# Splitting the partial sums of layer 0 between TensorE and VectorE 8 : 8, and moving the harmonics into a PSUM bank

## The reference

```python
# layer 0
h = relu(edge_feat @ W1 + b1)
w = (h @ W2 + b2).reshape(e, 4, 8, 8)          # four 8x8 matrices per edge
s_e, v_e = s[src], v[src]                      # 8 scalars and 8x3 vectors
m0 = ALPHA * (einsum('ei,eio->eo', s_e * sh0, w_000)
              + C110 * einsum('eim,em,eio->eo', v_e, sh1, w_110))
m1 = ALPHA * (einsum('ei,em,eio->eom', s_e, sh1, w_011)
              + einsum('eim,eio->eom', v_e * sh0, w_101))
out = segment_sum(m, dst) + self interaction
x = layernorm(x + out)
```

## Time and profile before

| | |
|---|---|
| median of 3 runs | 4191.23 us (4188.38 to 4191.39) |
| profiled execution | 4180.82 us |
| its span | 4179.0 us |
| mean granted TensorE clock | 0.938 |
| busy: PE, DVE, POOL, ACT | 86%, 79%, 72%, 53% |

### The profile page before, as it was taken

The page is one execution under the profiler, slowest core; times in us unless marked ns, Lnnn a source line. Parts: engine busy times, 40 slices in busy tenths (PEclk is TensorE's granted clock), DMA queues, the critical chain, the costliest instruction groups (busy, mean ns, idle before and its releaser), DMA issues.

```text
span 4179.0 us, 79599 instructions
## 1 busy us (share of the span) xinstructions
PE 3584.4 (86%) x24746; PEld 2173.1 (52%) x24746; DVE 3311.0 (79%) x5246; ACT 2201.5 (53%) x6573; POOL 3017.6 (72%) x3143
## 2 busy tenths in 40 slices
PE   5888888888888888888649999999999999999995
PEld 3555555555555555555425555555555555555553
DVE  7777777777777777777749988888888889888887
ACT  3555555555555555555325555555555556555553
POOL 5777777777777777777367777777777777777772
PEclk8999999999999999999879999999999999999998
DMA  3111111111111111111132212121212212121212
GB/s 103 33 29 33 29 33 29 34 33 29 33 29 33 29 33 29 33 31 31 18 48 47 46 39 47 37 47 37 47 37 47 47 37 48 37 47 37 47 37 32
DMA packets 220966, 159.83 MB, mean 38 GB/s; under 512 B 125489, under 2 KB 194994, under 8 KB 220466
## 3 DMA queue, kind: packets, MB, share of 16 engines
q0 software_dynamic: 100352, 51.58, 8.8%
q1 hardware_dynamic: 84946, 90.16, 8.2%
q10 hardware_dynamic: 35650, 17.88, 1.6%
HBM read 148.94 MB, written 10.43 MB: 38 GB/s over the span
## 4 chain that ended last, share of the span: by engine, by line
POOL 58%; issue 25%; PE 7%; DVE 6%; DMA 3%; DVEq 1%; POOLq 0%; ACT 0%; SPq 0%; ACTq 0%
POOL rows L364 58%; PE red L687 4%; PE wps L674 2%; DMA rows<-x_rows,src 2%; DVE prod L984 1%; DVE q L1036 1%; DMA src<-in_src 1%; PE wps L667 1%; DVE t_a L1022 0%; DVEq L1064 0%; DVE table L1060 0%; POOLq L381 0%; DMA x_rows<-table 0%; PE acc L701 0%; DMA rows<-in_x,src 0%
## 5 line engine op out<-in xcount | busy, mean ns | idle before, releaser
L364 POOL DMA_INDIRECT rows<-x_rows,src x1568 | 1504.6, 960 | 567.2 <-issue 562.7
L364 POOL DMA_INDIRECT rows<-in_x,src x1568 | 1512.1, 964 | 507.9 <-issue 498.5
L687 PE MATMUL red<-prod,ident 128*128 128x336 f32 (+2 forms) x6272 | 1753.6, 436 | 0.0
L687 PEld LDWEIGHTS red<-prod,ident 128*128 128x128 f32 x6272 | 1145.9, 193 | 651.1 <-issue 189.5
L493 ACT ACTIVATE gap<-iota,slot_plan 128x128 bf16<-128x128 f32 x3136 | 943.7, 387 | 85.3 <-DVE t_b L1087 76.0
L984 DVE TENSOR_TENSOR prod<-wps,q 128x896 f32<-128x896 f32 x784 | 836.3, 1084 | 191.2 <-PE wps L674 175.9
L667 PE MATMUL wps<-bias_parts,ones 64*128 64x448 bf16 (+1 forms) x2352 | 463.6, 391 | 517.4 <-DVE prod L978 324.4
L674 PE MATMUL wps<-w_sb,hidden 64*128 64x256 f32 (+1 forms) x4704 | 903.8, 487 | 0.0
L511 ACT ACTIVATE sums<-red 128x336 f32<-128x336 f32 (+2 forms) x392 | 168.6, 430 | 1084.1 <-PE red L687 1083.1
L667 PEld LDWEIGHTS wps<-bias_parts,ones 64*128 64x128 bf16 x2352 | 114.5, 94 | 1039.6 <-DVE prod L978 422.1
L674 PEld LDWEIGHTS wps<-w_sb,hidden 64*128 64x128 f32 x4704 | 487.5, 204 | 70.4 <-issue 25.6
(11 more groups left out here) (125 smaller groups left out, 3117.4 us busy)
## 6 DMA issues: line engine op xcount, KB each, us to landing
mlp<-in_dist SPq DMA_DIRECT2D x196, 256.0 KB
mlp<-in_feat SPq DMA_DIRECT2D x98, 256.0 KB
rows<-in_x,src POOLq DMA_INDIRECT x1568
rows<-x_rows,src POOLq DMA_INDIRECT x1568
frames<-frame ACTq DMA_DIRECT2D x49, 144.0 KB
geo<-frames ACTq DMA_DIRECT2D x98, 72.0 KB
src<-in_src SPq DMA_DIRECT2D x196, 8.0 KB, 1.6
geo<-in_sh ACTq DMA_DIRECT2D x98, 32.0 KB, 1.7
```

The source lines that it names most:

```text
L364: nc.gpsimd.indirect_dma_start(out=rows[z][:, t, :], out_offset=None, in_=table_rows, in_offset=bass.IndirectOffsetOnAxis(ap=src_sb[z][:, ...
L687: ins = nc.tensor.matmul(red[:, bank * 512:bank * 512 + cols], ident[:], pr[:, i, :, a:b, :], start=(i == 0), stop=(i == MUL - 1))
```

## The change

In layer 0 PE now sums tiles 0 to 7 only, in one bank, and DVE sums tiles 8 to 15. The second bank of `red`, which layer 0 no longer uses for sums, holds the harmonics: ACT copies each slot's 64 columns there with `copy_geo`, as it did for layer 1's frames, and DVE reads them from there. `load_geo` waits for that copy in place of DVE's last use; the copy waits for the load and for DVE's last use, and stands between the second half of the distances and the one-hots. DVE's first body waits until both slots are copied. Layer 1 keeps its split (12 : 4), its two banks and its place for the frames. `make_frames` stays where it is.

```diff
-PE_SUMS = (((0, 8), (8, 12)), ((0, 6), (6, 12)))
-PE_TILES = 12
-DVE_TILES = TILES - PE_TILES
-BANKS = 2
+PE_SUMS = (((0, 8),), ((0, 6), (6, 12)))
+PE_TILES = (8, 12)
+BANKS = (1, 2)
...
-        geo_ps = [hps[:, z * TILES * GEO[1]:(z + 1) * TILES * GEO[1]] for z in range(RING)]
-        red = psum("red", [P, BANKS * 512])
+        red = psum("red", [P, 2 * 512])
+        geo_ps = [[bank[:, z * TILES * GEO[n]:(z + 1) * TILES * GEO[n]] for z in range(RING)]
+                  for n, bank in enumerate((red[:, 512:1024], hps))]
...
-                act.wait_ge(s.geo_used[z] if n == 0 else s.geo_copied[z], r)
+                act.wait_ge(s.geo_copied[z], r)
...
-            def copy_geo(z, r):
+            def copy_geo(n, z, r):
-                s = layers[1]
+                s = layers[n]
                 act.wait_ge(s.geo_loaded[z], r * 16 + 16)
                 act.wait_ge(s.geo_used[z], r)
-                nc.scalar.activation(geo_ps[z], geo_sb[z][:], ACT.Copy).then_inc(s.geo_copied[z], 1)
+                nc.scalar.activation(geo_ps[n][z], geo_sb[z][:, 0:TILES * GEO[n]], ACT.Copy).then_inc(s.geo_copied[z], 1)
...
                     if n == 0:
+                        if not last:
+                            copy_geo(n, z, r + 1)
                         if not tail:
                             one_hots(n, z1, steps)
                             copy_sums(n, z1, r1, 0)
-                            copy_sums(n, z1, r1, 1)
...
                         weigh(n, z1, r1, range(2, H))
                         sum_products(n, z1, r1, 0)
-                        sum_products(n, z1, r1, 1)
...
             def harmonics(z):
-                return geo_sb[z][:, 0:TILES * GEO[0]].rearrange("p (t c) -> p t c", c=GEO[0])
+                return geo_ps[0][z].rearrange("p (t c) -> p t c", c=GEO[0])
...
-                if n == 0:
-                    dve.wait_ge(s.geo_loaded[z], r * 16 + 16)
-                else:
-                    dve.wait_ge(s.geo_copied[z], r + 1)
+                dve.wait_ge(s.geo_copied[z], r + 1)
...
             def prologue0(r, st):
+                dve.wait_ge(layers[0].geo_copied[1], r + 1)
```

More of the change, by code:

```diff
@@ L228, in __init__ @@
                 self.weights_used = ring("weights_used", HALVES[n])
-                self.products_summed = ring("products_summed", BANKS)
-                self.sums_copied = ring("sums_copied", BANKS)
+                self.products_summed = ring("products_summed", BANKS[n])
+                self.sums_copied = ring("sums_copied", BANKS[n])
                 self.messages_ready = ring("messages_ready")
@@ L252, in products @@
         def products(n):
-            return prod[:, 0:PE_TILES * PATHS[n] * MM].rearrange("p (i h t c) -> p i h t c", i=MUL, h=2 - n, t=PE_TILES)
+            return prod[:, 0:PE_TILES[n] * PATHS[n] * MM].rearrange("p (i h t c) -> p i h t c", i=MUL, h=2 - n, t=PE_TILES[n])
         def products_oi(n):
-            return prod[:, PE_TILES * PATHS[n] * MM:TILES * PATHS[n] * MM].rearrange(
-                "p (h t c i) -> p h t c i", i=MUL, h=2 - n, t=DVE_TILES)
+            return prod[:, PE_TILES[n] * PATHS[n] * MM:TILES * PATHS[n] * MM].rearrange(
+                "p (h t c i) -> p h t c i", i=MUL, h=2 - n, t=TILES - PE_TILES[n])
         def summed_by_dve(n, q):
-            return q * HALF_TILES[n] >= PE_TILES
+            return q * HALF_TILES[n] >= PE_TILES[n]
         def sums_by_half(n, z):
@@ L509, in copy_sums @@
                 cols = (b - a) * PATHS[n] * MUL
-                act.wait_ge(s.products_summed[z], r * BANKS + bank + 1)
+                act.wait_ge(s.products_summed[z], r * BANKS[n] + bank + 1)
                 nc.scalar.activation(sums_by_half(n, z)[:, :, a:b, :],
@@ L555, in body @@
                             hide(n, z, r + 1, 0)
-                            copy_geo(z, r + 1)
+                            copy_geo(n, z, r + 1)
                             hide(n, z, r + 1, 1)
@@ L574, in loop @@
                         load_geo(n, z, z, r0)
-                    if n == 1:
-                        for z in range(RING):
-                            copy_geo(z, r0)
+                    for z in range(RING):
+                        copy_geo(n, z, r0)
                     for z in range(RING):
@@ L590, in loop @@
                         copy_rows(n, 0, 1, r0)
-                    for bank in range(BANKS):
+                    for bank in range(BANKS[n]):
                         copy_sums(n, 0, r0, bank)
@@ L684, in sum_products @@
                 pe.wait_ge(s.weights_used[z], r * HALVES[n] + -(-b // HALF_TILES[n]))
-                pe.wait_ge(s.sums_copied[1 - z], (r + z) * BANKS - (BANKS - 1 - bank))
+                pe.wait_ge(s.sums_copied[1 - z], (r + z) * BANKS[n] - (BANKS[n] - 1 - bank))
                 for i in range(MUL):
@@ L945, in harmonics @@
             def harmonics(z):
-                return geo_sb[z][:, 0:TILES * GEO[0]].rearrange("p (t c) -> p t c", c=GEO[0])
+                return geo_ps[0][z].rearrange("p (t c) -> p t c", c=GEO[0])
             def frames(z):
-                return geo_ps[z].rearrange("p (t f m) -> p t f m", t=TILES, m=3)
+                return geo_ps[1][z].rearrange("p (t f m) -> p t f m", t=TILES, m=3)
             def sums_of(n, z, half=0):
@@ L963, in multiply @@
                 if oi:
-                    d0 = t0 - PE_TILES
+                    d0 = t0 - PE_TILES[n]
                     out = [products_oi(n)[:, h, d0:d0 + T].rearrange("p t (a o) i -> p t a o i", o=MUL)
@@ L992, in sum_tiles @@
                 dve.wait_ge(s.weights_used[z], r * HALVES[n] + HALVES[n])
-                st.done(nc.vector.tensor_reduce(sums_by_half(n, z)[:, :, PE_TILES:TILES, :], products_oi(n), AX_X, ALU.add))
+                st.done(nc.vector.tensor_reduce(sums_by_half(n, z)[:, :, PE_TILES[n]:TILES, :], products_oi(n), AX_X, ALU.add))
             def cut_message(n, z, r):
@@ L1085, in body0 @@
                 along = t_b[:, 0:TILES * 3 * MUL].rearrange("p (t o m) -> p t o m", t=TILES, m=3)
-                dve.wait_ge(s.sums_copied[z], r * BANKS + BANKS)
+                dve.wait_ge(s.sums_copied[z], r * BANKS[0] + BANKS[0])
                 nc.vector.tensor_tensor(
@@ L1136, in body1 @@
                 st.need(0)
-                dve.wait_ge(s.sums_copied[z], r * BANKS + BANKS)
+                dve.wait_ge(s.sums_copied[z], r * BANKS[1] + BANKS[1])
                 pair = sm[:, :, 0:4, :].rearrange("p t (b a) o -> p t b a o", a=2)
```

## The result

The changed kernel's median is 4170.5 us against 4191.4 us, a ratio of 0.9946 (95% interval 0.9932 to 0.9959). Run a second time it had 4164.7 against 4183.1 us, 0.9957 (0.9943 to 0.9970). The ratio and its interval leave out one slow run of the changed kernel, 15718.6 us at a granted clock of 0.191. The forecast was 4176, in a range of 4162 to 4192. The profiled execution took 4169.8 us (span 4168.0), 11.0 less than the profiled one of before.

What follows compares the result with a forecast made beforehand. POOL's gathers were taken to bound layer 0; -17 us of collisions + 1.6 us at the layer's end = -15.4 us, taking the median 4191.2 to 4175.8 us (-0.37%), range 4162 to 4192.

Steps and rivals of the forecast that it cites:

- The bound: Layer 0: POOL's gathers set the pace, 16 x 1.248 = 19.97 us a chunk, while DVE waits for rows.
- The operands: Layer 0: four DVE instructions reading harmonics from PSUM stop delaying gathers; 24.0 us of collisions removed, net gain 17 us.
- Rival B: Layer 0's second gather is slowed by the rows' arrival, not operands; only 2.8 us go, time 4190, chance 0.06.
- 1119.12: Layer 0 gather starting 0.02 us after L1018 takes only 0.95 us: the DVE instruction must already be running.
- What is left: Layer 0's remaining overlong gathers: 9 us, from L1091 (0.054 us per chunk) and grazes (0.03); bounds 0 and 26.
- rival C: Layer 0: L999 or L1005 falls on a gather every chunk if DVE's chain shifts over 0.2 us; 4205, chance 0.07.
- DVE's slack: Layer 0's frame chunk: DVE takes 18.7 us against 19.97, 1.3 us to spare; even late it wouldn't hold POOL.
- The sum of 8 tiles: DVE's reduce L993 in layer 0 grows from 1.752 to 3.35 us, 1.60 more, hidden by its wait for rows.
- The layer's end: At layer 0's end nothing covers DVE's longer sum: +1.6 us once, 0 if the 2.00 us wait absorbs it.
- TensorE: Layer 0: PE sheds one bank, 2.7 us per chunk, its wait growing to about 6.1; value 0, clock the risk.
- ScalarE: Layer 0: ACT swaps a 192-column copy for a 64-column one; moved waits fit its 4.08 us wait; value 0.
- The sum against the median: Whole run: 15.4 us saved, so 4165.4 from the profiled 4180.8 and 4175.8 from the median 4191.2.

Runs made afterwards that it cites:

- the 15-gather pair: Kernel before and changed kernel, each with 15 of 16 gathers per chunk in layer 0: 4101.3 us (0.9802) and 4073.2 us (0.9733).
- the harmonics-alone kernel: Kernel before with harmonics in PSUM, sums still 12 : 4, TensorE's second run reusing the first bank after ScalarE's copy: 4181.7 us, 0.9996.
- the shifted kernel: Changed kernel plus one unused DVE reduce of 256 constant columns before L1091 in each layer 0 body: 4178.4 us, 0.9987.

## Why the prediction was right

*The bound.* Right. With 16 gathers a chunk POOL's gathers set the pace of layer 0 in every kernel here, and its idle time from 80 us on is 487 to 489 us in all ten; a backlog of DVE is paid once, at the layer's end. With 15 gathers POOL began to wait for others.

*The operands.* Right, and the main term: 17 us forecast, 18.3 and 20.2 measured as the fall of the excess. Rival B, the landing, fell with the 44 second gathers that start inside L1014 and take no longer than 0.957 us. The Trainium skill (SBUF — State Buffer, "Who interferes with whom") says that a VectorE instruction with two SBUF inputs contends with a GpSimd instruction that reads SBUF. The traces agree, with the 1511 and 14303 gathers counted above, and the 15-gather pair tests the same four instructions in other phases: 32.3 us with two SBUF inputs, 0 with one. The measurement adds that the instruction must be running when the gather starts, as the forecast had read from 1119.12. The edge is sharp to some 0.04 us only: in the kernel before 14 gathers (1.6 us) start in the last moments of the reduce L993 and are held up by `add_window` (L1060) behind it, though some start up to 0.02 us ahead of that, as here:

```profile
86.09 1.06 POOL L364 DMA_INDIRECT rows<-in_x,src  x1 [0.30 <-issue]
86.11 0.57 DVE L1060 TENSOR_TENSOR table<-table,split 128x64 f32 x2
```

*What is left.* 9 us forecast, 7.7 and 5.8 measured, but not where I said. The addition of sums (old L1091) made 1.1 and 1.0 us instead of 5, because only the chunks on time met it. L998 (the old L999), which I had put safely between gathers, made 2.7 and 2.1 us with 8 and 6 gathers, all in late chunks: rival C's collision, in a few chunks. So the nearness of 9 and 7.7 is in part luck: the largest part of the 9 was five times too large, and others that the sum left out filled the place.

*DVE's slack.* This step was wrong. "After: 17.09 + 1.60 = 18.7 against a chunk of 19.97, 1.3 us to spare." In that chunk DVE has none to spare: L1014 starts 2.24 us (median) after the end of the last gather in every second chunk, 1.45 in the others, so DVE is 0.8 us late there. I had read the idle 3.41 us in front of L1018 as wait for rows, but 2 us of it is the body's own start. The 2.00 us in front of 1119.10 was the sign: a wait that returns as 1.97, 1.99 and 2.00 is no wait for data. L1060 of the changed kernel loads four window offsets into registers there. Its instructions (ns, min/median/max) in the changed kernel:

```profile
L1060 DVEq FUSED_REGOPS  x888: 75/183/211, 68.7 to 4133.4; - x178
L1060 DVEq SEQ_ASSERT  x792: 23/23/33, 68.9 to 4133.6; - x198
L1060 DVEq TENSOR_LOAD <-offs x198: 339/344/377, 68.3 to 4132.1; - x198
```

They are 888/198 = 4.5 register operations of 0.183, four checks of 0.023 and one load of 0.344 per body, 1.26 us, and they are not counted as busy. What fills the 2 us beyond that stays open. The step's second half held, "even a late DVE would not hold POOL"; but lateness moves the phases, and with the operands in SBUF that alone cost 12 us (an excess of 38.1 in place of 26.0). That the forecast held in spite of this step is luck, and the other half of the change saved it: with the operands in PSUM the late chunks made few collisions.

*The sum of 8 tiles.* 3.34 us against 3.35. *The layer's end.* +1.6 forecast, +2.0 and +1.7 measured; the 2.00 us wait stayed beside it.

*TensorE.* Right in its value of 0. PE's wait did not grow by 2.7 us a chunk, though: in the stretch it went from 281.5 us, as this line of the kernel before shows, to 425.0, 1.7 us a chunk. The clock probably takes the rest. Windows of the changed kernel (PE's busy time, count, then the granted clock), and behind them two of the kernel before:

```profile
PE wps L667 <- DVE prod L978: 281.5, 135, 4.6
```

```profile
1004.90:1008.50 3.60, 0.00 (x0) 0.90 0.17 28
1008.90:1012.30 3.40, 3.32 (x18) 0.50 0.45 142
1012.30:1015.70 3.40, 3.40 (x12) 0.67 0.11 15
1015.70:1019.10 3.40, 3.40 (x12) 1.00 0.06 10
```

```profile
1019.30:1022.60 3.30, 3.21 (x16) 0.53 0.56 175
1022.60:1029.40 6.80, 6.80 (x30) 1.00 0.10 15
```

Behind an idle 3.6 us PE runs at 0.50, the 1.2 GHz level, for 3.4 us and for two thirds of the next 3.4, which make 0.67 on average; in the kernel before the low clock ended with the first of its windows. The run's mean clock fell from 0.938 to 0.901, and DVE has no wait for PE in the stretch. The Trainium skill (TensorE: Matmul & The Clock Gate, "Why this matters for your kernels") advises against idle gaps between bursts of matmuls, because they bring the clock down. The trace agrees that the clock was low behind the gap; here it cost no time.

*ScalarE.* Right: in the same stretch DVE has no wait for ScalarE's copies.

*The sum against the median.* 20.9 and 18.5 us by the medians, 11.0 and 17.1 by pairs of profiled executions. Part of the first is layer 1's scatter. The rest stays open: of the kernel before, the profiled execution was the quickest in both series (4180.8 and 4181.1 us, with medians of 4191 and 4187), and no trace shows the others.

*The interaction.* The two halves don't add: the split alone costs 14 to 15 us, the harmonics alone gain nothing that can be told from noise in the form in which I built it (0.9987 to 1.0005), and together they gain 18 to 21. With the harmonics in SBUF the split makes DVE late and puts L1044 on a gather; in the harmonics-alone kernel PE could not spare the time that the split frees. Not tried: 12 : 4 with a PSUM bank of its own for the harmonics, since all eight are in use, nor with the harmonics in the columns that the 192 sums leave free in the second bank. So what the harmonics bring without the split is shown by the excess only.

## What to carry to other kernels

When POOL issues indirect DMAs back to back, look at the spread of their durations, not at the median: 17 ns on the mean of 1530 gathers was 26 us, and the list of DVE instructions running at the start of the long ones named the operands to move. Such collisions are a matter of phase. A chain that starts at the landing of the last gather is locked to the next ones, so a small shift on an engine with time to spare lost 13 us here, and two edits must be measured together as well as apart. Before counting idle time as slack, look for a length that repeats: it may be the engine's own sequencer.

## What the runs showed of the hardware beyond that

- A gather waits for a DVE instruction with both inputs in SBUF if that one runs at the gather's start (1511 of 1511 in twelve traces, 0 of 14303 where one input is in PSUM); it then ends about 0.82 us after the instruction's end (0.82 at 1015.84, 0.83 at 1031.62 above, 1018.38 + 1.34 - 1018.89 = 0.83 in the shifted kernel).
- POOL pauses for about 2 us before every 112th gather in both kernels (13 times, 21.6 and 21.4 us in layer 0). With 15 gathers a chunk neither kernel had such a pause in layer 0: no gap from 200 to 1900 us that the profile puts down to issue is over 0.4 and 0.7 us, and the longer ones end with ACT's q (up to 1.33) or the index load (up to 1.85). The cause was not looked for.
- The start of a DVE body, in which four window offsets are fetched into registers, takes 2 us in which the busy time shows nothing (idle 1.97 in front of 1025.69).
